# Causal attention and a gated LoRA layer on one core: products of values two stretches behind the scores, and four more tiles of a head group summed by GpSimd

## The reference

```python
q = (x @ wq).reshape(b, s, NH, HD)          # NH = 32 heads, HD = 32
k = (x @ wk).reshape(b, s, NKV, HD)         # NKV = 8 key heads, each shared by 4 heads
v = (x @ wv).reshape(b, s, NKV, HD)
...
scores = jnp.einsum('bihd,bjhd->bhij', q, k) * SCALE
scores = jnp.where(causal, scores, jnp.finfo(scores.dtype).min)
attn = jax.nn.softmax(scores, axis=-1)
out = jnp.einsum('bhij,bjhd->bihd', attn, v)
```

## Time and profile before

| | |
|---|---|
| median of 3 runs | 3460.47 us |
| profiled execution: its time | 3461.34 us |
| profiled execution: span of its instructions | 3459.6 us, granted PE clock 0.997 |
| attention | about 546 to 2575 us of the span |
| PE busy | 98% of the span; 1730.7 us of those 1747 |
| POOL busy | 51% of the span; 1565.6 of the 1747 us from 703 to 2450 us (groups 1 to 14) |
| ACT busy | 1024.7 us of those 1747 |
| DVE busy | 1239.2 us of those 1747 |

### The profile page before, as it was taken

How to read it: one execution, slowest core, us unless ns; L and a number is a source line. 1 busy time by engine, 2 the same in 40 slices (tenths; PEclk the granted TensorE clock), 3 DMA queues, 4 the chain that set the end, 5 groups by cost and what they waited for, 6 DMA issues and landing times.

```text
span 3459.6 us, 61790 instructions
## 1 busy us (share of the span) xinstructions
PE 3405.6 (98%) x25202; PEld 2389.0 (69%) x25202; DVE 2002.3 (58%) x3617; ACT 1467.6 (42%) x1830; POOL 1747.4 (51%) x749
## 2 busy tenths in 40 slices
PE   8999999999999999999999999999999999999998
PEld 7888886565665665666666566556558888878887
DVE  3122116777677677677777767767746766642222
ACT  3111112555665565565565556556553223211111
POOL 0000003888988998898898898889540000000000
PEclk9999999999999999999999999999999999999999
DMA  6334344021111111211112111110037777655553
GB/s 217 112 125 124 114 135 97 22 55 50 32 46 50 38 38 50 51 30 48 50 33 53 50 35 43 50 40 10 26 113 239 232 234 229 220 203 167 170 174 132
DMA packets 248556, 340.60 MB, mean 98 GB/s; under 512 B 55648, under 2 KB 150368, under 8 KB 248288
## 3 DMA queue, kind: packets, MB, share of 16 engines
q1 hardware_dynamic: 248288, 336.87, 32.6%
HBM read 203.08 MB, written 133.17 MB: 97 GB/s over the span
## 4 chain that ended last, share of the span: by engine, by line
PE 77%; POOL 18%; ACT 2%; DVE 2%; issue 1%; DMA 0%; POOLq 0%; ACTq 0%; SPq 0%; DVEq 0%
POOL p_psums L694 16%; PE p_acc L42 13%; PE p_o L771 12%; PE p_acc L44 12%; PE p_acc L43 12%; PE p_qm L722 11%; PE p_km L764 8%; PE p_km L757 2%; DVE p_part_max L883 1%; POOL p_psums L690 1%; ACT p_probs L847 1%; PE p_ag_ps L1198 1%; PE p_qm L726 1%; PE p_km L759 1%; PE p_acc L1187 1%
## 5 line engine op out<-in xcount | busy, mean ns | idle before, releaser
L883 DVE TENSOR_REDUCE p_part_max<-p_qm 128x1 f32<-128x512 f32 (+3 forms) x2240 | 1400.7, 672 | 556.0 <-PE p_qm L722 348.4
L694 POOL TENSOR_TENSOR p_psums<-p_psums,p_probs 128x1024 f32<-128x1024 f32 x620 | 1480.3, 2388 | 92.5 <-ACT p_probs L847 2.9
L847 ACT ACTIVATE p_probs<-p_km 128x1024 f32<-128x1024 f32 x896 | 887.6, 1023 | 463.1 <-PE p_km L764 451.7
L722 PE MATMUL p_qm<-p_k_st,p_q_st 96*128 96x512 f32 (+3 forms) x2560 | 907.8, 415 | 10.3 <-ACT p_neg_max L829 4.5
L722 PEld LDWEIGHTS p_qm<-p_k_st,p_q_st 96*128 96x128 f32 x2560 | 473.9, 191 | 255.7 <-issue 93.2
L764 PE MATMUL p_km<-p_q_st,p_k_st 97*128 97x512 f32 x1792 | 602.8, 418 | 12.6 <-ACT p_probs L847 8.3
L771 PE MATMUL p_o<-p_probs,p_v 128*32 128x256 f32 (+1 forms) x9216 | 566.6, 372 | 0.0
L771 PEld LDWEIGHTS p_o<-p_probs,p_v 128*32 128x32 f32 x9216 | 271.1, 110 | 222.1 <-issue 52.3
L764 PEld LDWEIGHTS p_km<-p_q_st,p_k_st 97*128 97x128 f32 x1792 | 311.3, 192 | 101.2 <-ACT p_probs L847 59.9
L690 POOL TENSOR_TENSOR p_psums<-p_probs 128x1024 f32<-128x1024 f32 x110 | 261.9, 2381 | 189.2 <-ACT p_probs L847 189.2
L679 POOL MEMSET p_k_st<- 1x2048 f32 x2 | 3.6, 1805 | 511.6 <-PE p_acc L44 511.6
(11 more groups left out here) (153 smaller groups left out, 3980.9 us busy)
## 6 DMA issues: line engine op xcount, KB each, us to landing
p_q_st<-q_hi SPq DMA_DIRECT2D x128, 256.0 KB, 4.7
p_x_raw<-in_xT SPq DMA_DIRECT2D x64, 256.0 KB, 3.5
q_hi<-p_out_hi SPq DMA_DIRECT2D x64, 256.0 KB, 2.0
q_lo<-p_out_lo SPq DMA_DIRECT2D x64, 256.0 KB, 2.4
p_q_st<-q_lo SPq DMA_DIRECT2D x64, 256.0 KB, 4.4
attended_T<-p_o_raw SPq DMA_DIRECT2D x128, 128.0 KB
p_a_raw<-attended_T SPq DMA_DIRECT2D x32, 512.0 KB, 9.7
p_recip<-reciprocals SPq DMA_DIRECT2D x128, 128.0 KB, 6.9
```

The costliest lines, as they stand in the source:

```text
L694: pool.tensor_tensor(sums[:, :, :], sums[:, :, :], probs[(n * NS + s) % PB][:, :, :], ALU.add).then_inc(added, 1)
L722: last = pe.matmul(bank[:, x * keys:(x + 1) * keys], q_st[par][0:ROWS, c, h + x, sub * P:(sub + 1) * P], k_st[par][0:ROWS, j * CK:j * CK + ...
L847: act.activation(tile[:, :, :].rearrange("p h q -> p (h q)"), km[s % 2][:, :, :].rearrange("p a b -> p (a b)"), ACT.Exp, scale=SCALE).then ...
L883: dve.reduce_max(part_max[c][:, h:h + heads, sub, j], qm[bank_of(i)][:, 0:item_width(i)].rearrange("p (h k) -> p h k", h=heads), AX.X).the ...
```

## The change

A constant `LAG` = 2 is added and put wherever visits were one stretch behind the scores. PE now does the scores of stretch sl and then visits stretch sl - 2; in the first two stretches of a group it visits the last two of the group before. ACT's copies, and SP's stores and loads of values, follow by the same step. And POOL's plan `POOLED` gets one more tile in each of chunks 3, 5, 6 and 7: 58 tiles instead of 54, 51 additions instead of 47. `LAST_SUMS`, the number of buffers and the order of scores and items stay.

```diff
+    LAG = 2
...
-    POOLED = [0, 3, 5, 6, 8, 9, 11, 12]
+    POOLED = [0, 3, 5, 7, 8, 10, 12, 13]
...
-                for sl, (c, steps) in enumerate(SLOTS[:-1]):
+                for sl, (c, steps) in enumerate(SLOTS[:-LAG]):
                     if steps[-1] + 1 == FIRST_STEP[c + 1]:
-                        events.append((SLOTS[sl + 1][1][-1] + 0.9, "store o", c))
+                        events.append((SLOTS[sl + LAG][1][-1] + 0.9, "store o", c))
...
-                    if sl > 0:
-                        values(n, par, sl - 1, plan)
+                    if sl >= LAG:
+                        values(n, par, sl - LAG, plan)
                     elif n > 0:
-                        values(n - 1, 1 - par, NSL - 1, SUMS)
+                        values(n - 1, 1 - par, NSL + sl - LAG, SUMS)
...
-            values(NG - 1, 1, NSL - 1, LAST_SUMS)
+            for sl in range(NSL - LAG, NSL):
+                values(NG - 1, 1, sl, LAST_SUMS)
...
-                    if sl > 0:
-                        c, done = SLOTS[sl - 1]
+                    if sl >= LAG:
+                        c, done = SLOTS[sl - LAG]
                         if done[-1] + 1 == FIRST_STEP[c + 1]:
                             output(n, c, plan)
-                    elif started:
+                    elif started and sl == LAG - 1:
                         output(n - 1, NC - 1, SUMS)
```

More of the change, by code:

```diff
@@ L601, in group @@
                 if started:
-                    events.append((SLOTS[0][1][-1] + 0.8, "store o before", NC - 1))
+                    events.append((SLOTS[LAG - 1][1][-1] + 0.8, "store o before", NC - 1))
                     if more:
-                        events.append((SLOTS[0][1][-1] + 0.9, "load v", 0))
+                        events.append((SLOTS[LAG - 1][1][-1] + 0.9, "load v", 0))
                 if last:
```

## The result

The changed kernel took 3531.41 us (median of 4 runs, 3530.67 to 3534.19) against 3460.38 for the one before on the same chip. The ratio on record is 1.0211, with a 95% interval of 1.0199 to 1.0224; the two medians alone give 1.0205. The profiled execution took 3530.67 us, its instructions 3528.9.

The account below looks back on a forecast made before the run. PE bounds the kernel before, POOL the changed one: 14 cycles of 130.3 instead of 124.45 us add 81.9, the ends -1.7 and +2.4. With 3461.3 that is 3543.9, as median 3543 us; 8-in-10 range 3508 to 3560.

Parts of the forecast that it names:

- POOL becomes the bound: Per group: 51 additions on POOL need 127.55 us without a wait, 5.2 us more than PE needs.
- The lag's part: Within a group: scores run further ahead, so POOL never has to wait; the lag can give only that.
- The handover: At a group's start: POOL's chunk 1 waits for PE's product of chunk 7's sum, 3.12 us in place of 2.35.
- The stalls: PE waits for POOL's sums in each group: 1.7 us at chunk 6 and some 4.3 us at chunk 7.
- the clock's cost at chunk 3: PE at half clock behind chunk 7's stall makes POOL wait 2.0 us at chunk 3, cycle 130.3 us.
- a margin of 0.4 us: At chunk 3: its second exponential is ready at 14.5 us, POOL needs it at 14.9.
- the sign of it: POOL idle 1 to 2.5 us before chunk 3's first addition, released by ACT, and nearly nowhere else.
- The ends: Outside the 14 cycles: -1.7 us from group 0, +2.4 us for PE working cold in the last group.
- The clock without effect: Rival 1: clock stays full or chunk 3's margin is 3 us; cycle 128.3, total 3513 us; chance 0.28.
- A quicker POOL: Rival 3: additions within a chunk follow at 2.35 us, PE bounds at 122.3 a group, 3429 us; chance 0.04.
- Rival 2: No margin at chunk 3, 3.2 us lost each time, a second clock fall; 3560 us; chance 0.13 with rival 4.
- rival 4: At group start POOL still waits for v17, chunk 1's exponentials behind it; 3565 us; chance 0.13 with Rival 2.

Follow-up runs that it names:

- the stalls filled: Changed kernel plus PE products of zeros before both stalls in groups 1 to 14 (3 at chunk 6, 7 at chunk 7): 3515.37 us, ratio 1.0164.
- 9 products filled in: Changed kernel plus 9 PE products of zeros per group before chunk 7's last products: 3523.70 us, ratio 1.0194 to the kernel before.

## Why the prediction was right, and where its sizes were off

**POOL becomes the bound.** Right: 51 additions, as far apart as before, POOL waiting 2.2 us in a group. The cycles with 56 and 57 tiles are 2.4 us apart, those with 57 and with 58 and the stalls filled 2.8; an addition is 2.525.

**The lag's part.** Right: it frees POOL of the waits for exponentials at the start. What it is worth with 58 tiles is shown by the run without it, 3628.6 us.

**The handover.** Right in kind. Its size was 0.75, measured 0.87 at full clock and 1.31 at half. I had the product in it but let the clock's loss begin behind it; the clock was already down when the product ran.

**The stalls.** 4.3 us at chunk 7 was forecast and 4.17 came; 1.7 us at chunk 6 and 1.10 came, since PE still was late from the cold start there: it had lost 1.46 us (below) and POOL 0.89, and 1.7 less the difference of 0.57 is 1.1.

**The term that was mis-sized** is the clock's cost at chunk 3: "I take the middle, 2.0 us", between 2.8 and 1.3, with a margin of 0.4 us. Measured 0.89, below both, and below the 1 to 2.5 us that were named as the sign of it. Of 6.8 us at half speed 1.4 fell into the stall, where nothing is lost, and 1.0 on the product; 4.4 us were left for s2, which at double length would be a loss of 2.2. But s2 took 1493.24 - 1488.12 = 5.12 us instead of 3.66, a loss of 1.46. (v0, s3, v1 and the part of s4 came as summed from the earlier trace rows: the second exponential of chunk 3 was there 15.96 us behind the start of s2, instead of 14.5.) Two things are in the 0.7 us that were not lost. In s2 at full clock PE waited 0.29 us for a negated maximum, which the sum had counted as work, and at half clock it did not wait. And at half clock what follows a pair of score products started 0.85 us after it (1488.72 to 1489.57) instead of 0.47 (1460.79 to 1461.26), 1.8 times and not double.

The one cold border of the run with both stalls filled shows the other case: the fall came behind the stall, all 6.8 us fell on work, and POOL waited 2.05 us. By this one border 2.0 is what a fall costs that meets only work, and the error was above all where it falls.

With 0.89 instead of 2.0 at chunk 3 and 0.56 more at the handover, the cycle is 129.7, not 130.3: measured 129.58, so 0.7 us in 14 cycles, 10 us of the 13 between the forecast for the profiled execution, 3543.9, and its 3530.7. The ends make the other 3.

**The ends.** +2.4 us was forecast for group 15 and -1.8 came, where the kernel before had lost its clock three times by short waits for ACT (rows 11 shows one) and the changed one lost it once behind the cold start, though PE's waits for ACT in that stretch are the same in both, 8.3 us in 17 pieces. In group 0 -0.65 came for -1.7. (A clock of 0.97 in rows 11 puts that fall at 2511.94 us and not at 2511.97; nothing hangs on it.)

**The rivals.** The clock without effect (3513) fell with the trace's cold borders; the run with both stalls filled, 3515 us, shows that it would have come out about there. A quicker POOL did not show. Rival 2 needed 3.2 us at chunk 3, where 0.89 came; and against rival 4, POOL waited at the border for PE's product and not for an exponential.

The rule of the Trainium skill that was weighed, in "TensorE: Matmul & The Clock Gate" ("HAM oscillation — how this bites in real kernels"), is that every wait of sufficient length starts the next burst cold. This case agrees for stalls of 4.1 to 4.2 us, at 13 borders of 13 looked at. For shorter stalls the runs show both outcomes.

## What to carry to other kernels

An engine that is just quick enough has a need that can be counted: instructions per period times their distance, taken from starts and not from lengths. Before moving work onto it, compare that count with the period; here, behind the longer lag, two tiles more were a gain of 7 to 10 us and four a loss of 80. Deeper lag turned POOL's scattered waits into slack in one piece, which more additions could use. And where the new bound leaves PE standing for microseconds, look at what the granted clock does behind the stall: here it cost 1.0 us of each group on top.

## What the runs showed of the hardware

Adding PE work made a kernel faster: 3531 to 3515 us with 4.3 us more per group, because the clock stayed up. Stalls of 4.1 to 4.2 us lowered it every time. For shorter ones the length does not tell: with 9 products filled in, the clock fell behind 6 of 13 stalls at chunk 6 (1.54 to 2.00 us) and not behind one of 1.93; with 57 tiles behind three of 1.54 to 1.71 us and not behind one of 1.74; with lag 1 it stayed up behind 2.6 us at chunk 7. GpSimd's additions of 128x1024 fp32 came 2.525 us apart where each reads the sum just written and waits at a semaphore for it, and 2.33 to 2.35 where the next one was independent; no run tells the reading from the waiting.
